# The router product with the router's columns stationary, and the dense lists made anew

## The chip, the cores and the metric

One Trainium2 chip; the kernel runs on one of its NeuronCores. The metric is the device time of one execution in microseconds. TensorE multiplies, VectorE, ScalarE and GpSimd (POOL in the profile) do the elementwise work, SyncE (SP) issues most DMAs. Each engine takes its instructions strictly in the order of its own program and waits at semaphores for the others.

## The reference

Two transformer layers over x of 4 x 1024 tokens and 256 columns, all float32, here cut to what matters:

```
xn = layernorm(x)
x1 = x + attention0(xn) + relu(xn @ W1 + b1) @ W2 + b2      # the dense stage: 4 batches
xn = layernorm(x1)
scores = softmax(xn @ Wg.T)                                  # the router: 256 -> E = 8 logits a token
weights, experts = top_k(scores, 2); weights /= weights.sum()
moe = sum over the 2 chosen experts of weight * LoRA-SwiGLU(xn, expert)
out = x1 + grouped_attention1(xn) + moe
```

The router's logits decide which rows go to which expert, so the rows are scattered into slots, sorted by expert, before the experts run.

## The kernel before

The program has four stages: dense (stage 0), the first half of the second layer's attention (1), the experts (2), and the second half of the attention (3). What each engine does is cut into *units*, such as `RL:2`, and each engine has a list of them: `LAYER0_UNITS` for the dense stage, `ATTENTION_UNITS` for the attention. The dense lists are cyclic. `layer0_order` goes through a list once per turn, for turns -1 to 4; a unit with no mark belongs to the batch of the turn, one with `+` to the next batch, one with `-` to the one before. So the units with `+`, all in the last part of the list, open the kernel in turn -1. Between two stages the lists are joined: `AHEAD` says how many units of the next stage go behind each named unit of the last batch. No engine looks past a unit that waits.

TensorE's dense units: `XT` turns two tiles of xn; `PT` the product of wq.wk with xn; `VV` values of two tiles; `S` scores of one tile, `TP` turned probabilities, `AV` probabilities by values, `LT` and `FC` the output product; `W1` (16 per batch) and `W2` (8 per batch) the FFN; `EP` half of an expert's LoRA fold. `RT` turns two tiles of the second layernorm's output, `RL` makes the router's logits of these two tiles. Each `x + y` product that is not the router's is made of three fp32r products of high and low parts (helper `times`, L549). The turned tiles go through two PSUM banks T, the products through four banks G, in the order of TensorE's list: a bank can be written again when the unit that used it four products before has been evicted.

The router's path in a pair of tiles: VectorE's `N1` normalizes two tiles (L934) when GpSimd's `X1` has its root; TensorE's `RT` turns them (L709); ScalarE's `RT` copies the bank to `xn1T` (L726), which is a single buffer, when TensorE has finished the previous `RL`; TensorE's `RL` (L718) makes four f32 products, for each tile and each of the two column blocks, with the turned tile stationary and the router's 8 columns moving; VectorE's `RL` copies 16 columns to `logit` and finds the top two (L955 to L961). `TK` and `TG` make indices and gates, `CH` in stage 1 counts the slots.

At the start, GpSimd's `FA` splits an expert's LoRA factors, which SP's `LL` has loaded; SP's `LL:1` waits for `FA:0`. In the first batch `FA:1` goes on with the low parts of the two FFN weights: W1's (L523, signal `ffn_split` 1), then W2's (L525, signal 2). TensorE's `W1:0` of the first batch waits for signal 1, ScalarE's `W1:0` for signal 2. GpSimd's `XT` adds a bias row to two tiles (L517). SP's `CL` clears three slots with zeros (385.5 KB, 24 in all), which must be over before the scatter.

At the join, GpSimd's `ES` makes the low part of a folded expert matrix (L532) from ScalarE's `EL`, SP's `SM` stores the matrix (L457), `SX` and `SN` store x1 and xn. SP's `LC:1` loads the rotation table `turn` (L1273) behind the last `SM`; VectorE's `OF:0` (L1611) waits for it. In stage 1 GpSimd's `SC` scatters one tile of rows to the slots with two indirect DMAs (L1347), `YS` takes a root for an output tile when VectorE has its variance, `LE` loads the first expert.

## Time and profile before

| | |
|---|---|
| median of 3 runs | 1117.2 us (1113.53 to 1121.52) |
| the profiled execution | 1116.3 us, span 1114.6 us |
| mean granted clock | 0.974 of full speed |
| TensorE busy | 1055.8 us, 95% of the span |
| VectorE busy | 781.8 us, 70% |
| GpSimd busy | 434.6 us, 39% |
| ScalarE busy | 393.5 us, 35% |
| chain that ended last | TensorE 87%, VectorE 4% |

A busy TensorE is one that has a product in flight; the ends of products are modelled. In the chain of waits, "issue" and "another core or an unknown queue" are time for which the profile shows no releaser. The granted clock has two levels, full (2.4 GHz) and half (1.2 GHz); a value between them is a stretch that had both. The kernel is one long sequence, so a stretch of the span is a stage: dense to about 430 us, the first attention half to about 620, the experts to about 970, the second half to the end.

### The profile page before, as it was taken

What the parts mean: (1) busy time and instruction counts of PE and PEld (TensorE: products, weight loads), DVE (VectorE), ACT (ScalarE), POOL (GpSimd) and SP (SyncE); (2) the same over time, 40 slices, a digit from 0 to 9 for tenths busy, and PEclk for the clock granted to TensorE, in tenths of its full rate; (3) what the DMA queues carried; (4) which work ended last, traced back from release to release, by engine and by line L of the source; (5) the groups of instructions that cost most, each with busy time, mean ns of one, the idle gap of its engine ahead of it and who ended that gap; (6) DMA issues with size and microseconds to landing.
All of it is one profiled execution on the core that took longest, in us unless ns stands there. A gap on an engine that the chain in (4) does not pass through costs nothing.

```text
span 1114.6 us, 20433 instructions
## 1 busy us (share of the span) xinstructions
PE 1055.8 (95%) x6338; PEld 915.2 (82%) x6338; DVE 781.8 (70%) x1741; ACT 393.5 (35%) x770; POOL 434.6 (39%) x416
## 2 busy tenths in 40 slices
PE   5999999999999996995899899999999999999995
PEld 4899999999999996864677788888888888877874
DVE  5688787878788676754565777777777777764745
ACT  2636463555446363431211222222222222442300
POOL 2846454555447331045575100000011010088886
PEclk8999999999999998897899999999999999999998
DMA  9364672666468346425466446534355252265456
GB/s 272 97 206 130 187 244 101 192 160 202 140 190 205 123 148 185 126 76 171 151 189 214 166 136 223 171 116 142 101 194 166 78 194 58 84 123 86 68 95 141
DMA packets 113780, 168.61 MB, mean 151 GB/s; under 512 B 17296, under 2 KB 87568, under 8 KB 113552
## 3 DMA queue, kind: packets, MB, share of 16 engines
q1 hardware_dynamic: 93328, 120.09, 35.5%
q0 software_dynamic: 20352, 47.23, 15.3%
...
## 4 chain that ended last, share of the span: by engine, by line
PE 87%; DVE 4%; issue 2%; another core or an unknown queue 2%; DMA 2%; SPq 1%; POOL 1%; ACT 0%; DVEq 0%; POOLq 0%; ACTq 0%
PE wide L549 19%; PE wide L1900 17%; PE bank L549 11%; PE bank L1900 9%; PE wide L1398 7%; PE bank L1398 3%; PE bank L1925 3%; PE wide L1458 3%; PE wide L1482 2%; PE bank L1482 2%; PE bank L640 1%; PE bank L1893 1%; PE wide L1471 1%; PE wide L1468 1%
## 5 line engine op out<-in xcount | busy, mean ns | idle before, releaser
L1900 PE MATMUL wide<-expert_ring,xsT 128*128 x642 | 170.5, 401 | 3.1 <-DVE xsT L1989 2.3
L1900 PEld LDWEIGHTS wide<-expert_ring,xsT 128*128 128x128 f32 x642 | 113.3, 188 | 23.4 <-issue 3.9
L1958 ACT ACTIVATE gsT<-bank 128x512 fp32r<-128x512 f32 x71 | 42.5, 599 | 242.3 <-PE bank L1925 242.3
...
L2001 DVE TENSOR_TENSOR slots_h<-wide,expert_bias 128x512 f32<-128x512 f32 x71 | 49.1, 691 | 68.0 <-PE wide L1900 67.8
L1347 POOL DMA_INDIRECT slot_rows_scratch<-ring,slot x64 | 69.2, 1081 | 52.0 <-DVE slot L1734 32.0
L532 POOL TENSOR_TENSOR folded_matrix<-fold,folded_matrix 128x512 fp32r<-128x512 f32 x48 | 64.0, 1341 | 42.5 <-ACT folded_matrix L726 39.7
L549 PE MATMUL wide<-xnT,w 128*128 128x512 f32 x234 | 60.3, 399 | 0.0
L1900 PEld LDWEIGHTS bank<-expert_ring,gsT 128*128 128x128 f32 x432 | 56.1, 189 | 3.5 <-issue 0.3
L944 DVE TENSOR_TENSOR hT<-hid,hT 128x512 fp32r<-128x512 f32 x64 | 54.6, 860 | 5.9 <-ACT hid L781 5.1
L549 PE MATMUL wide<-xnT,pT 128*128 128x512 f32 (+2 forms) x288 | 58.6, 348 | 0.0
L529 POOL TENSOR_TENSOR rsa<-vea,half 128x1 f32<-128x1 f32 x32 | 21.3, 666 | 95.3 <-DVE vea L908 94.3
L1900 PE MATMUL bank<-expert_ring,xsT 128*128 x210 | 57.5, 409 | 0.1
L1900 PE MATMUL bank<-expert_ring,gsT 128*128 x432 | 57.3, 281 | 0.1
L1900 PEld LDWEIGHTS wide<-expert_ring,gsT 128*128 128x128 f32 x420 | 54.2, 188 | 3.0
L1989 DVE TENSOR_TENSOR gsT<-bank,gsT 128x512 fp32r<-128x512 f32 x71 | 49.1, 691 | 9.9 <-ACT gsT L1958 0.5
L549 PE MATMUL wide<-w,hT 128*128 128x256 f32 x456 | 55.7, 278 | 0.0
L1330 POOL DMA_INDIRECT first_half<-slot_results_scratch,slot x32 | 51.9, 1622 | 9.2 <-issue 9.2
L1900 PE MATMUL wide<-expert_ring,gsT 128*128 x420 | 55.2, 280 | 0.0
L2010 DVE SCALAR_TENSOR_TENSOR slots_g<-slots_h,xs_ring,slots_h 128x512 f32<-128x512 f32 x71 | 53.4, 752 | 2.5
L549 PEld LDWEIGHTS wide<-w,hT 128*128 128x128 f32 x456 | 54.5, 188 | 0.4
L1330 POOL DMA_INDIRECT x1b<-slot_results_scratch,slot x16 | 26.0, 1626 | 73.4 <-DVE x1b L1650 68.9
...
## 6 DMA issues: line engine op xcount, KB each, us to landing
...
slot_rows_scratch<-zeros SPq DMA_DIRECT2D x23, 385.5 KB, 7.5
...
```

The costliest lines, as they stand in the source:

```text
L532: tt(fold_part(n, 1), fold[:, n % 2, :], fold_part(n, 0), ALU.subtract).then_inc(matrix_ready, 1)
L549: ins = mm(o, stationary(i), moving(j), start=(first and q == 0), stop=(last and q == 2))
L944: tt(hT[:, 1, n % IC, :], hid[:, n % 2, :], hT[:, 0, n % IC, :], ALU.subtract).then_inc(hid_low, 1)
L1330: nc.gpsimd.indirect_dma_start(out=target, out_offset=None, in_=scr["ys"], in_offset=index(k, tile_at), bounds_check=SLOTS - 1, compute_op ...
L1347: nc.gpsimd.indirect_dma_start(out=scr["xs"], out_offset=index(k, n), in_=ring[:, n % RINGS, k * ROW:(k + 1) * ROW], in_offset=None, bound ...
L1398: ins = mm(o, stationary(i), moving(j), start=(first and k == 0), stop=(last and k == 2))
L1482: last = mm(o[:, 0:DIM], oT[:, h % 2, e, n % 4 * P:(n % 4 + 1) * P], wo1[:, e, :], start=(e == 0), stop=(e == EC - 1))
L1900: ins = mm(o, parts[i], moving, start=(first and q == 0), stop=(last and q == 2))
L1958: return nc.scalar.activation(o, i, ACT.Copy)
L1989: tt(flat[1], bank, flat[0], ALU.subtract).then_inc(taken, 1)
L2001: tt(h1[:, j % 2, :], H[j % 2][0], bias(e, 0, HID), ALU.add).then_inc(h1_ready, 1)
L2010: stt(out=g[:, i, :], in0=h1[:, i, :], scalar=xs[:, j % ROUND, DIM:ROW], in1=h3[:, i, :], op0=ALU.mult, op1=ALU.mult).then_inc(g_ready, 1)
```

## The change

RT now lays the turned tiles by column block, both tiles side by side. RL makes two f32 products, each with 8 of the router's columns stationary and the two turned tiles (256 columns) moving; the result is 8 x 256, logits turned. ScalarE has a new unit RL: it copies these to `xn1T`'s first 8 partitions. TensorE has a new unit RB: it turns them back, two blocks of 8 x 128, into columns 256 to 271 of the same bank. VectorE's RL and ScalarE's next RT wait for RB instead of RL. All dense lists, the lists of the first attention half and the joins have a new order: `W1:0+` stands eighth among the units that open TensorE's program (it was seventeenth), the clears move from one turn before to one turn behind their batch, GpSimd's first YS stands behind SC:7 instead of SC:10. The diff (of the attention lists only GpSimd's is shown):

```diff
--- before.py
+++ after.py
@@ -47,34 +47,35 @@
 
 LAYER0_UNITS = {
     "tensor": """
-        RL:3- W1:6 S:5 FC:1 LT:2 EP:4 W1:7 AV:3 TP:4 FC:2 S:6 EP:5 W2:0 LT:3 AV:4 W2:1 TP:5 FC:3 W2:2 EP:6 W2:3
-        LT:4 W1:8 EP:7 AV:5 TP:6 S:7 W1:9 W1:10 FC:4 LT:5 W1:11 W1:12 AV:6 TP:7 EP:8 W1:13 W1:14 W1:15 FC:5 LT:6
-        XT:0+ EP:9 AV:7 EP:10 XT:1+ FC:6 W2:4 LT:7 EP:11 W2:5 VV:0+ PT:0+ W2:6 PT:2+ EP:0+ XT:2+ FC:7 W2:7 XT:3+
-        RT:0 VV:1+ EP:1+ S:0+ RL:0 S:1+ RT:1 PT:1+ VV:2+ TP:0+ PT:3+ RL:1 W1:0+ S:2+ RT:2 AV:0+ TP:1+ W1:1+ S:3+
-        LT:0+ W1:2+ EP:2+ RL:2 W1:3+ AV:1+ TP:2+ VV:3+ EP:3+ S:4+ RT:3 FC:0+ W1:4+ LT:1+ W1:5+ AV:2+ TP:3+
+        W1:4 LT:1 AV:2 W1:5 FC:1 TP:3 LT:2 EP:2 S:5 W1:6 EP:3 AV:3 TP:4 W1:7 FC:2 S:6 EP:4 LT:3 AV:4 W2:0 EP:5
+        TP:5 W2:1 FC:3 W2:2 LT:4 EP:6 RL:3- AV:5 RB:3- W2:3 TP:6 EP:7 W1:8 FC:4 W1:9 S:7 W1:10 W1:11 LT:5 W1:12
+        AV:6 TP:7 EP:8 W1:13 W1:14 W1:15 FC:5 LT:6 EP:9 AV:7 XT:0+ W2:4 XT:1+ FC:6 W2:5 VV:0+ LT:7 EP:10 W2:6
+        XT:2+ FC:7 W2:7 PT:0+ XT:3+ EP:11 PT:2+ RT:0 W1:0+ EP:0+ VV:1+ S:0+ RL:0 EP:1+ RT:1 VV:2+ RB:0 S:1+ PT:1+
+        TP:0+ S:2+ W1:1+ AV:0+ PT:3+ RL:1 TP:1+ RT:2 S:3+ RB:1 W1:2+ LT:0+ AV:1+ RL:2 RT:3 W1:3+ RB:2 VV:3+ TP:2+
+        S:4+ FC:0+
     """,
     "scalar": """
-        W1:5 TP:3 EL:3 W1:6 LT:2 EX:5 W1:7 TP:4 EL:4 LT:3 EL:5 TP:5 LT:4 EX:6 W1:8 TP:6 EL:6 EL:7 W1:9 W1:10 LT:5
-        EX:7 W1:11 W1:12 TP:7 W1:13 W1:14 EL:8 LT:6 W1:15 XT:0+ EL:9 XT:1+ LT:7 VV:0+ GX:0- EL:10 PT:0+ EL:11
-        PT:2+ XT:2+ XT:3+ RT:0 VV:1+ EL:0+ EX:0+ RT:1 PT:1+ TP:0+ VV:2+ PT:3+ EX:1+ W1:0+ EL:1+ RT:2 TP:1+ W1:1+
-        EX:2+ W1:2+ LT:0+ EX:3+ TP:2+ W1:3+ VV:3+ RT:3 EL:2+ LT:1+ W1:4+ EX:4+
+        W1:3 LT:1 W1:4 EX:4 TP:3 W1:5 LT:2 EL:2 W1:6 EX:5 TP:4 W1:7 LT:3 EL:3 TP:5 EL:4 EX:6 RL:3- EL:5 LT:4 TP:6
+        W1:8 W1:9 EL:6 EL:7 W1:10 LT:5 EX:7 W1:11 W1:12 TP:7 W1:13 W1:14 W1:15 LT:6 XT:0+ XT:1+ EL:8 EL:9 LT:7
+        VV:0+ GX:0- XT:2+ PT:0+ EL:10 XT:3+ PT:2+ RT:0 EL:11 W1:0+ VV:1+ RL:0 EX:0+ RT:1 VV:2+ TP:0+ PT:1+ EX:1+
+        EL:0+ W1:1+ RL:1 TP:1+ PT:3+ RT:2 EX:2+ W1:2+ LT:0+ RL:2 RT:3 EX:3+ EL:1+ VV:3+ TP:2+
     """,
     "vector": """
-        AV:2 W1:4 RL:3- W1:5 TP:3 S:5 FC:1 LT:2 EP:4 SA:2 W1:6 W1:7 TP:4 ST:0+ AV:3 SA:3 ST:1+ FC:2 S:6 EP:5 LT:3
-        AV:4 W2:0 ST:2+ W2:1 TP:5 FC:3 W2:2 EP:6 ST:3+ VA:0+ LT:4 EP:7 W2:3 SA:4 AV:5 X1:0 TP:6 W1:8 S:7 SA:5
-        FC:4 W1:9 LT:5 W1:10 NM:0+ W1:11 AV:6 W1:12 EP:8 TP:7 SA:6 W1:13 W1:14 FC:5 LT:6 EP:9 W1:15 TK:0- XT:0+
-        AV:7 EP:10 X1:1 SA:7 FC:6 W2:4 XT:1+ LT:7 EP:11 NM:1+ W2:5 N1:0 VV:0+ PT:0+ N1:1 W2:6 EP:0+ PT:2+ XT:2+
-        X1:2 FC:7 W2:7 TG:0- XT:3+ X1:3 S:0+ VV:1+ S:1+ EP:1+ RL:0 PT:1+ N1:2 TP:0+ VV:2+ PT:3+ RL:1 S:2+ AV:0+
-        W1:0+ N1:3 SA:0+ TP:1+ S:3+ EP:2+ RL:2 W1:1+ LT:0+ AV:1+ F1:0 W1:2+ TP:2+ EP:3+ VV:3+ FC:0+ W1:3+ S:4+
-        SA:1+ LT:1+
+        VV:3 TP:2 S:4 FC:0 LT:1 AV:2 SA:2 W1:3 FC:1 EP:2 W1:4 TP:3 LT:2 S:5 W1:5 AV:3 W1:6 ST:0+ EP:3 TP:4 W1:7
+        SA:3 FC:2 LT:3 AV:4 F1:0- EP:4 SA:4 S:6 ST:1+ W2:0 EP:5 TP:5 W2:1 FC:3 W2:2 EP:6 ST:2+ LT:4 ST:3+ RL:3-
+        X1:0 AV:5 W2:3 VA:0+ EP:7 TP:6 W1:8 FC:4 S:7 NM:0+ W1:9 W1:10 LT:5 SA:5 W1:11 AV:6 EP:8 W1:12 TP:7 W1:13
+        TK:0- W1:14 FC:5 W1:15 NM:1+ LT:6 EP:9 SA:6 X1:1 XT:0+ AV:7 W2:4 SA:7 FC:6 W2:5 XT:1+ LT:7 EP:10 VV:0+
+        TG:0- W2:6 FC:7 XT:2+ N1:0 X1:2 W2:7 N1:1 PT:0+ EP:11 PT:2+ EP:0+ X1:3 XT:3+ S:0+ W1:0+ VV:1+ EP:1+ RL:0
+        S:1+ VV:2+ TP:0+ PT:1+ N1:2 AV:0+ N1:3 S:2+ W1:1+ TP:1+ PT:3+ RL:1 S:3+ SA:0+ LT:0+ AV:1+ SA:1+ RL:2
+        W1:2+
     """,
     "gpsimd": """
-        ES:2 SA:1 ES:3 SA:2 FA:4 SA:3 ES:4 ES:5 SA:4 FA:5 ES:6 VA:0+ ES:7 XT:0+ SA:5 SA:6 ES:8 FA:0+ ES:9 X1:0
-        SA:7 X1:1 ES:10 ES:11 X1:2 X1:3 FA:1+ XT:1+ ES:0+ XT:2+ ES:1+ FA:2+ XT:3+ SA:0+ F1:0 FA:3+
+        FA:2 SA:2 FA:3 ES:2 ES:3 XT:2 SA:3 FA:4 ES:4 ES:5 XT:3 SA:4 VA:0+ ES:6 FA:5 ES:7 SA:5 FA:0+ F1:0- XT:0+
+        X1:0 SA:6 ES:8 ES:9 XT:1+ X1:1 SA:7 ES:10 X1:2 ES:11 X1:3 FA:1+ ES:0+ SA:0+ ES:1+ SA:1+
     """,
     "sync": """
-        LX:0+ LW:2 LW:3 SM:1 LL:4 LL:5 LW:4 SM:2 CL:0+ SX:0 SM:3 CL:1+ LW:5 LL:0+ CL:2+ CL:3+ SM:4 CL:4+ LW:0+
-        LL:1+ SM:5 SX:1 LL:2+ SN:0 SG:0- LW:1+ SM:0+ LL:3+ CL:5+ SN:1
+        LX:0+ SM:0 LW:2 LL:3 CL:0- LL:4 SM:1 LW:3 LW:4 LL:5 SM:2 SX:0 CL:1- LW:5 CL:2- LL:0+ SM:3 CL:3- SM:4
+        LW:0+ SX:1 LL:1+ CL:4- SM:5 CL:5- SN:0 LL:2+ LW:1+ SN:1 SG:0-
     """,
 }
 
@@ -339,7 +340,8 @@
     nmx = sb("nmx", [P, 2])
     rsum = sb("rsum", [P, 4])
     rinv = sb("rinv", [P, 4])
-    xrT = sb("xn1T", [P, 2, DC, P])
+    xrT = sb("xn1T", [P, DC, 2 * P])
+    turned_logits = xrT[0:E, 0, :]
     logit = sb("logit", [P, TPB, E])
     top = sb("top", [P, TPB, 8])
     topi = sb("topi", [P, TPB, 8], mybir.dt.uint32)
@@ -362,6 +364,7 @@
     gates_ready, gates_stored, diff_ready, ed_ready = (sem("gates_ready"), sem("gates_stored"), sem("diff_ready"),
                                                        sem("gate_exponents_ready"))
     varn_ready, r2_ready, g_step = sem("xn1_var_ready"), sem("r2_ready"), sem("gate_step")
+    logits_high, logits_done = sem("turned_logits_ready"), sem("logits_done")
     matrix_out, matrix_ready = sem("matrix_out"), sem("matrix_parts_ready")
     factors_ready = sem("factors_ready")
     p_step, p_held, v_held = sem("gpsimd_step"), keep["held"]["gpsimd"], keep["held"]["vector"]
@@ -706,18 +709,22 @@
                 o, done = t_free(u)
                 for t in range(2):
                     for c in range(DC):
-                        last = tr(o[:, (DC * t + c) * P:(DC * t + c + 1) * P], xb[:, b % 2, 2 * n + t, c * P:(c + 1) * P],
+                        last = tr(o[:, (2 * c + t) * P:(2 * c + t + 1) * P], xb[:, b % 2, 2 * n + t, c * P:(c + 1) * P],
                                   ident[:])
                 last.then_inc(done, 1)
             elif kind == "RL":
                 pe.wait_ge(late_in, 32)
                 pe.wait_ge(*taken_t((b, "RT", n)))
                 o, done = g_free(u)
+                for c in range(DC):
+                    last = mm(o[0:E, 0:2 * P], rout[:, c, :], xrT[:, c, :], start=(c == 0), stop=(c == DC - 1))
+                last.then_inc(done, 1)
+            elif kind == "RB":
+                pe.wait_ge(logits_high, TPB // 2 * b + n + 1)
                 for t in range(2):
-                    for c in range(DC):
-                        last = mm(o[:, t * E:(t + 1) * E], xrT[:, t, c, :], rout[:, c, :],
-                                  start=(c == 0), stop=(c == DC - 1))
-                last.then_inc(done, 1)
+                    last = tr(g_bank((b, "RL", n))[:, 2 * P + t * E:2 * P + (t + 1) * E], turned_logits[:, t * P:(t + 1) * P],
+                              ident[0:E, 0:E])
+                last.then_inc(logits_done, 1)
 
         return unit
 
@@ -782,8 +789,10 @@
             elif kind == "RT":
                 if TPB // 2 * b + n:
 
-                    act.wait_ge(g_done, G_AT[(b, "RL", n - 1) if n else (b - 1, "RL", TPB // 2 - 1)] + 1)
-                copy(xrT[:].rearrange("p t c q -> p (t c q)"), t_of(u)[:]).then_inc(taken_t(u)[0], 1)
+                    act.wait_ge(logits_done, TPB // 2 * b + n)
+                copy(xrT[:].rearrange("p c q -> p (c q)"), t_of(u)[:]).then_inc(taken_t(u)[0], 1)
+            elif kind == "RL":
+                copy(turned_logits, g_of(u)[0:E, 0:2 * P]).then_inc(logits_high, 1)
             elif kind == "GX":
                 act.wait_ge(diff_ready, b + 1)
                 if b:
@@ -951,8 +960,9 @@
                     dve.wait_ge(matrix_ready, q - 1)
                 tt(fold[:, n % 2, :], raw[:, m % 2, n % 2 * 512:(n % 2 + 1) * 512], o, ALU.add).then_inc(taken_g(u)[0], 1)
             elif kind == "RL":
-                o, pair = g_full(u), (2 * n, 2 * n + 1)
-                nc.vector.tensor_copy(logit[:, 2 * n:2 * n + 2, :].rearrange("p t e -> p (t e)"), o[:, 0:2 * E]).then_inc(taken_g(u)[0], 1)
+                o, pair = g_bank(u), (2 * n, 2 * n + 1)
+                dve.wait_ge(logits_done, TPB // 2 * b + n + 1)
+                nc.vector.tensor_copy(logit[:, 2 * n:2 * n + 2, :].rearrange("p t e -> p (t e)"), o[:, 2 * P:2 * P + 2 * E]).then_inc(taken_g(u)[0], 1)
                 hold(dve, v_held, *taken_g(u))
                 for t in pair:
                     last = nc.vector.max(top[:, t, :], logit[:, t, :])
...
     "gpsimd": """
-        SC:0 SC:1 SC:2 SC:3 SC:4 SC:5 SC:6 SC:7 SC:8 SC:9 SC:10 YS:0 LE:0 YS:1 SC:11 YS:2 SC:12 SC:13 SC:14 SC:15
-        SC:16 YS:3 SC:17 YS:4 SC:18 SC:19 SC:20 SC:21 YS:5 SC:22 YS:6 SC:23 YS:7 SC:24 SC:25 SC:26 LE:1 SC:27
-        SC:28 YS:8 LE:2 SC:29 SC:30 SC:31 YS:9 YS:10 YS:11 YS:12 YS:13 YS:14 YS:15
+        SC:0 SC:1 SC:2 SC:3 SC:4 SC:5 SC:6 SC:7 YS:0 SC:8 SC:9 SC:10 SC:11 SC:12 SC:13 SC:14 LE:0 SC:15 SC:16
+        SC:17 YS:1 YS:2 LE:1 SC:18 YS:3 SC:19 SC:20 YS:4 SC:21 YS:5 SC:22 YS:6 SC:23 YS:7 SC:24 SC:25 LE:2 SC:26
+        SC:27 SC:28 YS:8 SC:29 SC:30 SC:31 YS:9 YS:10 YS:11 YS:12 YS:13 YS:14 YS:15
     """,
...
@@ -1075,9 +1085,9 @@
 
 AHEAD = (
 {
-    "tensor": "W2:6:1 RT:0:1 RT:1:3 RT:2:1 RT:3:2",
-    "scalar": "LT:7:2 EL:10:1 EL:11:1 RT:0:3 RT:1:2 RT:2:1 RT:3:3",
-    "vector": "X1:2:2 W2:7:2 RL:0:2 N1:2:2 RL:1:1 N1:3:3 F1:0:2 TK:0:1",
+    "tensor": "FC:7:1 RT:0:1 RT:1:1 RB:0:1 RT:2:1 RT:3:1 RL:3:2",
+    "scalar": "LT:7:4 EL:10:1 RL:0:1 RT:1:1 RT:2:1 RL:2:2 RL:3:3",
+    "vector": "W2:5:1 EP:10:1 X1:2:1 X1:3:1 N1:3:4 RL:1:4 F1:0:1 TK:0:5",
     "gpsimd": "",
     "sync": "LW:5:1 SM:5:1",
 },
@@ -1085,7 +1095,7 @@
     "tensor": "YY:14:1 YY:15:29",
     "scalar": "GA:15:18",
     "vector": "YS:13:1 YS:14:2 YF:11:1 YS:15:4 YF:12:19 YF:13:1 YF:15:2",
-    "gpsimd": "YS:10:1 YS:13:1",
+    "gpsimd": "YS:12:1 YS:14:1",
     "sync": "RG:31:12",
 },
 {
```

The units that open the kernel, from these lists, and the join on VectorE and SP (`[1]` is stage 1, `3.` the last batch):

```
TensorE before: XT:0 XT:1 VV:0 PT:0 PT:2 EP:0 XT:2 XT:3 VV:1 EP:1 S:0 S:1 PT:1 VV:2 TP:0 PT:3 W1:0 S:2 AV:0 TP:1 W1:1
TensorE after:  XT:0 XT:1 VV:0 XT:2 PT:0 XT:3 PT:2 W1:0 EP:0 VV:1 S:0 EP:1 VV:2 S:1 PT:1 TP:0 S:2 W1:1 AV:0 PT:3 TP:1
GpSimd before:  VA:0 XT:0 FA:0 FA:1 XT:1 ES:0 ...     after: VA:0 FA:0 XT:0 XT:1 FA:1 ES:0 ...
SP before:      LX:0 CL:0 CL:1 LL:0 CL:2 CL:3 CL:4 LW:0 LL:1 ...     after: LX:0 LL:0 LW:0 LL:1 ...
VectorE join before: 3.W2:7 [1]WL:0 [1]OF:0 2.TG:0 3.X1:3 3.RL:0 [1]WL:1 [1]UT:1 3.N1:2
VectorE join after:  3.W2:7 3.N1:1 3.EP:11 3.X1:3 [1]OF:0 3.RL:0 3.N1:2 3.N1:3
SP join before: 3.SM:4 3.SM:5 [1]LC:1 3.SX:1 3.SN:0 2.SG:0 3.SN:1 3.SG:0
SP join after:  3.SX:1 2.CL:4 3.SM:5 [1]LC:1 2.CL:5 3.SN:0 3.SN:1 2.SG:0 3.CL:0 ... 3.CL:5 3.SG:0
```

## Rows read from the trace of the kernel before

**Rows 1.** Busy time by stretch, whole kernel; busy us and count per engine, clock, DMA.
```profile
100.00:200.00 100.00, 100.00 (x701) 92.98 (x700) 79.54 (x213) 49.92 (x99) 49.89 (x50) 1.00 0.54 169
440.00:450.00 10.00, 5.37 (x24) 4.97 (x25) 9.29 (x30) 1.39 (x3) 0.69 (x1) 0.50 0.54 128
500.00:510.00 10.00, 3.83 (x14) 2.91 (x14) 3.79 (x6) 0.00 (x0) 7.40 (x8) 0.67 0.73 204
510.00:520.00 10.00, 3.54 (x18) 2.60 (x17) 1.22 (x3) 2.37 (x5) 4.62 (x5) 0.84 0.59 176
520.00:530.00 10.00, 10.00 (x41) 8.05 (x41) 7.70 (x14) 2.16 (x5) 5.39 (x5) 0.80 0.47 155
550.00:560.00 10.00, 7.76 (x24) 6.28 (x25) 8.69 (x17) 4.13 (x7) 2.11 (x3) 0.66 0.27 70
```

**Rows 2.** Instructions in order, TensorE; start, length, what, idle before.
```profile
443.70 1.12 PE L709 MATMUL bank<-ident,u 128*128 128x128 f32 x4 [8.07 <-DVE u L934]
```

**Rows 3.** What TensorE waited for: us in total, times, longest.
```profile
PE bank L1482 <- issue: 6.2, 1, 6.2
PE wide L1398 <- DVE uT L1619: 4.7, 1, 4.7
PE bank L1482 <- DVE oT L1668: 3.8, 1, 3.8
```

**Rows 4.** Chain of waits, 130 to 180 us; start, us, what.
```profile
130.20 0.79 PE wide L718 x8
135.00 0.11 PE bank L640
135.11 1.38 PE bank L549 x6
```

**Rows 5.** Chain of waits, from 1000 us: another f32 product.
```profile
1016.18 1.73 PE bank L1482 x8
```

**Rows 6.** Instructions in order, GpSimd, start of the kernel.
```profile
16.24 1.52 POOL L517 TENSOR_TENSOR u<-u,crow 128x256 f32<-128x256 f32 x2 [3.71 <-DVE crow L824]
24.32 1.43 POOL L500 TENSOR_TENSOR lora_parts<-lora,lora_parts 32x512 fp32r<-32x512 f32 x1 [0.18 <-POOL lora_parts L499]
32.53 4.60 POOL L523 TENSOR_TENSOR w<-u,w 128x2048 fp32r<-128x2048 f32 x1 [0.26 <-POOL lora_parts L500]
37.10 4.65 POOL L525 TENSOR_TENSOR w<-w_raw,w 128x2048 fp32r<-128x2048 f32 x1
```

**Rows 7.** Instructions in order, TensorE, start of the kernel.
```profile
22.22 2.90 PE L549 MATMUL bank<-wv,xnT 128*128 128x256 f32 x12 [1.21 <-DVE xnT L843]
37.19 1.66 PE L549 MATMUL bank<-xnT,w 128*128 128x512 f32 x6 [0.62 <-POOL w L523]
41.70 1.54 PE L549 MATMUL wide<-xnT,pT 128*128 128x512 f32 x6
```

**Rows 8.** Instructions in order, ScalarE, start of the kernel.
```profile
41.85 0.69 ACT L780 ACTIVATE hT<-bank,cols 128x512 fp32r<-128x512 f32 x1 [4.19 <-POOL w L525]
```

**Rows 9.** Chain of waits, start of the kernel: SP and the LoRA load.
```profile
12.10 0.91 SPq L462
13.98 8.11 DMA lora<-in_expert_lora
```

**Rows 10.** Instructions in order, VectorE, start of the kernel.
```profile
22.59 2.03 DVE L872 TENSOR_SCALAR xp<-u,mv,rs 128x256 f32<-128x256 f32 x4
```

**Rows 11.** Instructions in order, VectorE, join: eviction of the last W2 unit.
```profile
429.53 0.42 DVE L920 TENSOR_TENSOR u<-u,wide 128x256 f32<-128x256 f32 x1 [1.02 <-PE wide L549]
```

**Rows 12.** Chain of waits, 400 to 640 us, at the join.
```profile
427.31 1.38 POOL folded_matrix L532
428.70 0.54 SPq L457
429.34 7.45 DMA turn<-in_turn
```

**Rows 13.** Costliest groups of the page: busy, mean ns, idle before.
```profile
L1347 POOL DMA_INDIRECT slot_rows_scratch<-ring,slot x64 | 69.2, 1081 | 52.0 <-DVE slot L1734 32.0
```

28 lines of the change are left out of this document (14 added, 14 removed).

## The prediction

> **What bounds the kernel now.** I read the busy shares of the engines by stretch first. From 100 to 200 us, well inside the dense stage, TensorE is busy for all of the 100 us at full clock while the other engines have room [rows 1], and I take that stretch for the whole middle of the dense stage. There only TensorE's own work counts: whatever adds to it is paid, and whatever other engines get more of is not, until it makes TensorE wait. Then I read its waits. Nearly all idle time lies at the edges: 8.1 us before the router's third turned pair of the last batch [rows 2], and 6.2, 4.7 and 3.8 us in the attention half behind it [rows 3]. After the first of these the granted clock is at half (1.2 GHz) in 440 to 450 us, and it is down again around the others [rows 1]. A new order of the dense lists can therefore gain only at the edges, and can lose anywhere.
>
> **The router's product.** Before, a unit RL is four f32 products, each moving 8 columns and loading 128 x 128: 8 records, 0.79 us in the chain of waits in mid-stage [rows 4]. The new RL is two products moving 256 columns, so 4 records. The nearest row is another f32 product of 256 moving columns: 8 records in 1.73 us, 0.216 each [rows 5]. Four make 0.86 us. The new RB turns two 8 x 128 blocks back. Bound from above: a 128 x 128 turn takes 0.11 us [rows 4], two are 0.22; from below: nothing. I take 0.20, because the loaded block still has 128 columns like that row. A unit goes from 0.79 to 1.06, +0.27; twelve units lie in the full stretch, **+3.2 us** (+0.9 to +3.5). The last four lie in the join, counted there. ScalarE gets 16 small copies; it is half idle in mid-stage [rows 1], so I cost them at nothing there; were that cover gone, the 0.3 to 0.6 us of each would stand in front of the next turned pair. VectorE's work is unchanged.
>
> The Trainium skill, "TensorE: Matmul & The Clock Gate", section on the back-to-back issue gap, gives 262 cycles for 256 columns, 0.109 us at 2.4 GHz, with no surcharge for f32. By that the product would cost 0.44 us. The trace's f32 row disagrees by a factor of two, and I go by the trace.
>
> **The start of the dense stage** is the largest term. A unit W1 of the first batch needs the low part of the first FFN weight, which GpSimd makes (L523, 32.53 us, 4.60 long), and ScalarE's W1 unit needs the second one too (L525, from 37.10, 4.65 long) [rows 6]. Before, W1:0 is seventeenth in TensorE's list; the engine comes to it at about 36.6 and starts at 37.19, barely late [rows 7]. ScalarE waits for the second part until 41.85 [rows 8], while TensorE goes on with what was ahead. In the new lists W1:0 stands eighth, right behind PT:2, on both queues. Behind it, in order, are now EP:0, VV:1, S:0, EP:1, VV:2, S:1, PT:1, TP:0 and PT:3, all of which ran ahead of it.
>
> When does the gate open? SP no longer issues two clears of the slots ahead of the first LoRA load. That load went out at 13.98 and landed 8.1 us later, at 22.1; the clears took SP from 12.10 [rows 9]. So it goes out 1.9 us earlier and has the data of two clears less ahead of it; I take a landing at 19.7 (18.0 to 20.5). FA:0 takes 3.7 us (22.1 to the end of L500 at 25.8), so to 23.4. Now both bias units (1.52 each) stand between FA:0 and FA:1: 26.4; one of them used to fill the wait ahead of FA:0 [rows 6]. FA:1 takes about as long as FA:0 less its queue time, 3.3, then L523: the first gate opens at 34.5 instead of 37.1, the second at 39.1 instead of 41.8.
> When does TensorE come to it? VectorE now normalizes the second half of the tiles (2.03 us, L872 [rows 10]) ahead of the first turned tiles, which moves VV:0 from 22.22 [rows 7] to about 24. VV:0, XT:2, PT:0, XT:3, PT:2 end near 30.2. So it idles 4.3 us there. Six records of 512 columns are 1.38 us in mid-stage [rows 4], twelve of 256 as many columns: W1:0, EP:0, VV:1, S:0, EP:1 (1.4, 0.24, 1.4, 0.7, 0.24) run to 38.5. VV:2 needs the bank that W1:0 filled, which ScalarE empties only at 39.1 + 1.3 = 40.4. From there VV:2, S:1, PT:1, TP:0, S:2, W1:1, AV:0, PT:3 and TP:1 are 8.1 us: 48.5. Before, the same set was done at 41.70 [rows 7]. The difference, **+6.7 us** (+4 to +9, by the landing and by whether the idling halves the clock), meets a stage with no idle time, so nothing gives it back.
>
> **The join with the attention half.** What SP does there matters. The last EP unit now stands behind W2:7, whose eviction on VectorE starts at 429.53 [rows 11], and ScalarE takes it behind RT:0; the split on GpSimd takes 1.38 [rows 12]. The last store of the expert matrix, 428.70 before, then goes out near 433.9, and the load of the rotation table, queued behind it, at 434.5 instead of 429.34. It took 7.45 us to land [rows 12]; so 441 to 442 instead of 436.8. VectorE's OF:0 waits for it with N1:2 and N1:3 queued behind, and the third RT waits for N1:2 as before. From that landing to the third RT VectorE needed 6.9 us (436.8 to 443.70 [rows 2, 12]); the gates, X1:3, a weight's low part and a UT unit no longer stand in between, which leaves 3.9 by my estimate: 445.4, 1.7 us later. RB:2 adds a step on the way to the last RT's copy and RL, 0.6 us, and UT:2 now runs after the wait, in the slow clock. **+3 us** (0 to +6). Six clears of the last batch move in front of its gates' store on SP; they are hidden behind the logits, unless the queue is still full there.
>
> **The scatter.** GpSimd's indirect writes, 1.08 us each [rows 13], ran 22 in a row before its first YS; the new list has 16, with YS:0 then holding GpSimd until the first output rows are there. In that burst TensorE, ScalarE and VectorE stand still with no releaser on record [rows 3]. I read it as other queues starved by the burst, but no row shows that. Bounds: all of the standing still goes (-21, below) or it grows by half as much (+8). I take **-2**, close to nothing since a shorter burst sometimes only moves the stall.
>
> **The sum**: 3.2 + 6.7 + 3 - 2 = +10.9 on the profiled execution's 1116.3 us, 1127. The median of the runs is 1117.2, so on that I am 0.9% slower.
>
> **Rivals.**
> - *The standing still in the scatter goes.* TensorE is busy for 3.83 and 3.54 us of the two stretches from 500 to 520 and 7.76 of 550 to 560 [rows 1]: 14.9 us idle. What it did there ran at clocks of 0.67, 0.84 and 0.66, and 10 us behind it at 0.80: 1.3 + 0.6 + 2.6 + 2.0 = 6.5 us more, 21 together. 1116.3 + 12.9 - 21 = 1108. This is the end on the other side, not slower, and it decides if the new position of YS:0 comes before the engines run dry. For it: each pause of GpSimd's burst is followed by a restart. Against: GpSimd's burst begins at about the same place.
> - *The start gate does not bite*, because the first LoRA load lands near 17 and its factors are done before TensorE arrives: 1116.3 + 3.2 + 3 - 2 = 1120.5. For it, the queue ahead of it shrinks; against, GpSimd has two more bias units in the way.
> - *The product is cheap.* If a product of 256 columns costs what an fp32r one of as many columns does (half of 1.38 / 6, 0.115), RL and RB are 0.66 us, 0.13 less than before: -1.6 instead of +3.2, 1122. It is what the skill's section above gives.
> - *The turn-back stalls mid-stage.* ScalarE's copy of the next turned pair waits for RB, and RB stands behind a whole VV:2, S:3 or W1:3. For 1.4 us ScalarE holds everything queued behind that copy. If TensorE runs out of evicted banks for 1 us per unit, twelve units cost +12: 1139. Against it, ScalarE's half idle time.
>
> **How the numbers follow.** The forecast's case (1119 to 1135 alone) has 0.42, the scatter 0.20, the open gate 0.15, the cheap product 0.07, the turn-back 0.16. What a measurement can tell from no change is about 1%, so 1106 to 1128. Slower by more: 0.2 of the forecast's case, 0.15 of the turn-back, 0.02 else: 0.37. Faster by more: half of the scatter's case less what sits inside, and what the new attention lists may bring beside it: 0.16. The rest 0.47. The range runs from the scatter's case to just under the turn-back's.
>
> **What would show it.** The product's line with four records and about 0.216 us each; two short records for the turning back. TensorE waiting on GpSimd's L523 or on W1's bank between 30 and 41 us, with W1:0 first and not after PT:3. The wait before the third RT at 9 to 10 us. TensorE busy for all of 60 to 430 still; idle time there is the fourth rival. The first long gap in the scatter shorter. It is wrong if the dense stage ends no later than before.

## The result, and the profile after

The changed kernel takes 1129.2 us, the median of 4 runs (1127.01 to 1130.52); the kernel before, beside it, 1119.0 (1113.53 to 1121.52). The ratio is 1.0104, with a 95% interval of 1.0085 to 1.0124. The forecast was 1127, in a range from the scatter's case (1108) to just under the turn-back's (1139). The profiled execution took 1128.95 us, with a span of 1127.2, against 1116.3 and 1114.6 before: 12.6 us of span to account for.

Busy time by stretch of the changed kernel, with the columns of [rows 1]:

```profile
20.00:30.00 10.00, 6.31 (x25) 5.75 (x26) 5.39 (x9) 5.87 (x8) 8.60 (x10) 0.66 0.13 45
30.00:40.00 10.00, 6.53 (x30) 5.52 (x29) 2.67 (x4) 1.80 (x4) 9.45 (x3) 0.83 0.25 82
100.00:200.00 100.00, 100.00 (x689) 89.28 (x688) 77.74 (x211) 48.50 (x99) 46.51 (x50) 1.00 0.46 152
450.00:460.00 10.00, 2.69 (x8) 0.70 (x7) 1.03 (x2) 2.03 (x5) 1.22 (x2) 0.81 0.85 273
460.00:470.00 10.00, 6.36 (x25) 4.16 (x25) 8.68 (x27) 3.46 (x7) 0.00 (x0) 0.50 1.13 259
```

The middle of the dense stage is still all TensorE, at full clock; the opening is now half idle and runs partly at 1.2 GHz (clock 0.66 and 0.83); the join from 450 us is poorer than [rows 1] showed it at 440. What TensorE waited for (us in total, times, longest), to be held against [rows 3]:

```profile
PE bank L712 <- DVE u L943: 10.5, 2, 10.0
PE wide L1408 <- issue: 4.2, 5, 2.1
PE bank L552 <- DVE xnT L852: 3.8, 1, 3.8
PE wide L552 <- POOL w L526: 3.5, 1, 3.5
PE bank L1423 <- issue: 2.9, 1, 2.9
```

Two of these waits lie in the opening. The one for the turned tiles (L852) was 1.21 us before [rows 7], the one for the weight's low part (L526) 0.62. The long waits behind the join, 6.2, 4.7 and 3.8 us, have become 4.2 in five pieces, 2.9, and 2.5 that ended with VectorE.

**The start**, instructions in order (start, length, what, idle before). They answer to [rows 6 to 8]:

```profile
23.69 2.90 PE L552 MATMUL bank<-wv,xnT 128*128 128x256 f32 x12 [3.81 <-DVE xnT L852]
30.57 4.53 POOL L526 TENSOR_TENSOR w<-u,w 128x2048 fp32r<-128x2048 f32 x1 [0.26 <-POOL lora_parts L503]
35.15 1.90 PE L552 MATMUL wide<-xnT,w 128*128 128x512 f32 x6 [3.47 <-POOL w L526]
39.80 0.69 ACT L787 ACTIVATE hT<-wide,cols 128x512 fp32r<-128x512 f32 x1 [7.48 <-POOL w L528]
41.21 1.60 PE L552 MATMUL wide<-wv,xnT 128*128 128x256 f32 x12 [0.25 <-ACT hid L788]
```

W1:0 starts at 35.15 with 3.47 us of idle time before it, and VV:2 at 41.21, when ScalarE has emptied W1:0's bank. The fourth score tile of batch 0, for which the same set of units has been done in both kernels, starts at 49.13 against 41.70 [rows 7]: **+7.4**. That is one profile against one. The six kernels that open exactly like the one before start this tile between 41.70 and 43.05, four of the five with the new opening between 49.13 and 49.48 and the fifth at 50.53, so a start is known to about 1 us.

**The stage** from there to the end of the last W2 unit (the start of TensorE's next record) takes 395.3 us (49.13 to 444.45) against 387.6 (41.70 to 429.33): **+7.7**. Kernels with the same lists and product repeat this length within 0.02 us. The new product and the turn back from 100 to 400 us, by shape (busy, mean ns, idle):

```profile
L720 PE MATMUL bank<-xn1T,router 128*8 128x256 f32 x24 | 6.2, 380 | 0.0
L725 PE MATMUL bank<-ident,xn1T 8*128 8x8 f32 x12 | 1.7, 212 | 0.0
L725 PEld LDWEIGHTS bank<-ident,xn1T 8*128 8x128 f32 x12 | 1.2, 135 | 2.2 <-issue 2.2
```

**The join.** TensorE in order, and the chain of waits (start, us, what):

```profile
462.69 1.11 PE L712 MATMUL bank<-ident,u 128*128 128x128 f32 x4 [10.00 <-DVE u L943]
466.15 1.87 PE L720 MATMUL wide<-xn1T,router 128*8 128x256 f32 x4 [0.73 <-issue]
```

```profile
449.29 1.28 POOL folded_matrix L535
450.59 0.55 SPq L460
451.24 7.67 DMA turn<-in_turn
```

The third turned pair waits 10.00 us, and the product behind it 0.73. The profile names no releaser for the 0.73; ScalarE's copy of the pair (465.45, 0.60 long) lies in it, and that copy had waited for the turn back, a step that the old product did not have. The pair starts 18.2 us behind the last W2 unit, 14.4 before [rows 2]. From that unit to the first product of an expert's weights it is 184.4 us against 187.2: **-2.8**. From there to TensorE's last product it is the same, 485.4 and 485.2. 7.4 + 7.7 - 2.8 is 12.3 of the 12.6; the rest lies behind.

Those 184.4 us hold a loss and a gain. Up to the first scatter they are 64.1 us against 57.3, with TensorE idle for 12.8 us against 9.0. From the first scatter to the experts they are 120.3 against 130.0, with the columns of [rows 1], the kernel before first:

```profile
486.59:616.57 129.98, 110.53 (x493) 83.94 (x492) 68.00 (x149) 22.61 (x40) 81.58 (x83) 0.92 0.57 174
508.54:628.86 120.32, 108.13 (x491) 80.71 (x490) 67.68 (x149) 20.37 (x34) 80.19 (x83) 0.97 0.62 188
```

TensorE's idle time there falls from 19.5 us to 12.2, and its mean granted clock rises from 0.92 to 0.97.

### The profile page after: what moved, and what is told of

Same layout as the page of the kernel before. It is cut to its first block, busy times and chain, and to the rows that moved or that the text cites. A ratio compares the mean times of both kernels' runs of the same rounds, so it can differ in the third digit from the quotient of the medians.

```text
span 1127.2 us, 20384 instructions
## 1 busy us (share of the span) xinstructions
PE 1066.7 (95%) x6306; PEld 906.2 (80%) x6306; DVE 776.4 (69%) x1741; ACT 397.6 (35%) x786; POOL 430.2 (38%) x416
## 3 DMA queue, kind: packets, MB, share of 16 engines
q0 software_dynamic: 20352, 47.23, 15.1%
## 4 chain that ended last, share of the span: by engine, by line
PE 89%; DVE 3%; issue 3%; POOL 2%; DMA 1%; SPq 1%; ACT 0%; DVEq 0%; POOLq 0%; ACTq 0%
PE wide L552 17%; PE wide L1910 17%; PE bank L552 13%; PE bank L1910 9%; PE wide L1408 7%; PE bank L1408 3%; PE bank L1935 3%; PE wide L1468 2%; PE wide L1492 2%; PE wide L1481 2%; PE wide L1478 2%; PE bank L1492 2%; PE bank L643 1%; PE bank L1903 1%; PE wide L720 1%
## 5 line engine op out<-in xcount | busy, mean ns | idle before, releaser
L552 PE MATMUL wide<-xnT,w 128*128 128x512 f32 x216 | 56.0, 398 | 3.5 <-POOL w L526 3.5
L552 PE MATMUL bank<-w,hT 128*128 128x256 f32 x480 | 59.1, 279 | 0.0
L1910 PE MATMUL bank<-expert_ring,gsT 128*128 x432 | 57.3, 281 | 0.1
L552 PEld LDWEIGHTS bank<-w,hT 128*128 128x128 f32 x480 | 56.8, 188 | 0.1
L552 PEld LDWEIGHTS wide<-xnT,pT 128*128 128x128 f32 x288 | 47.6, 189 | 6.3
```

Source lines behind the costliest of these rows:

```text
L552: ins = mm(o, stationary(i), moving(j), start=(first and q == 0), stop=(last and q == 2))
L1910: ins = mm(o, parts[i], moving, start=(first and q == 0), stop=(last and q == 2))
```

## The experiments

The kernel before gave 1117.5 us beside the first four kernels, 1100.7 beside the next four and 1101.4 beside the last four; these were three different chips. So every ratio is to the kernel before on the same chip, and stages are compared by their own length. "The rest" of a kernel is what it has over the kernel before, by its ratio, when the start and the stage of its profile are taken off; it is known no better than the start.

**1. The opening turn in its old order.**

```
+START = {"tensor": "XT:0 XT:1 VV:0 PT:0 PT:2 EP:0 XT:2 XT:3 VV:1 ... PT:3 W1:0 S:2 ...", "scalar": ..., "vector": ...}
     for turn in range(-1, BATCH + 1):
+        if turn < 0 and opening:
+            order += [(0, u.split(":")[0], int(u.split(":")[1])) for u in opening]
+            continue
```

> The changed kernel, but its opening turn (the units of batch 0 that run ahead of the first full turn) stands on TensorE, ScalarE and VectorE in the order of the kernel before; the rest of the lists and the new router product stay. Theory A (the start is the gate of the feed-forward weights, met too early): TensorE no longer waits 3.5 us on the low split of the weights, its 24 products of the first hidden tile no longer run at the low clock, and the same set of units is done about 7 us earlier; the time falls by 7 us to about 1122, a ratio of 1.003 to 1.005 to the kernel before. Rival B (TensorE's later units wait for the same VectorE and ScalarE work anyway, the gate only hides it): the time falls by 2 us at most, ratio 1.008 or more.

1122.16 us, ratio 1.0037 (1.0021 to 1.0053): 7.5 us under the changed kernel (1.0104 less 1.0037, of 1117.5). Its busy time in the opening:

```profile
20.00:30.00 10.00, 8.14 (x40) 6.89 (x40) 7.99 (x14) 7.25 (x9) 8.81 (x10) 0.83 0.11 36
30.00:40.00 10.00, 10.00 (x67) 9.20 (x66) 6.65 (x15) 6.38 (x16) 9.87 (x3) 1.00 0.25 84
```

The fourth score tile starts at 41.69, the stage takes 395.4. What the opening loses, nothing behind it gives back. Theory A holds, rival B falls.

**2. W1:0 alone moved back** (on TensorE, ScalarE and VectorE; TensorE's list is shown).

```
-"... XT:3 PT:2 W1:0 EP:0 VV:1 S:0 EP:1 VV:2 S:1 PT:1 TP:0 S:2 W1:1 ..."
+"... XT:3 PT:2 EP:0 VV:1 S:0 EP:1 VV:2 S:1 PT:1 TP:0 S:2 W1:0 W1:1 ..."
```

> The changed kernel with one unit moved: the first hidden tile W1:0 of the opening turn goes behind the third score row, just ahead of W1:1, on TensorE, ScalarE and VectorE. Theory A (that unit's gate alone makes the start late): within 1.5 us of the kernel whose whole opening turn is as before, so about 6 to 7 us under the changed kernel. Rival B (the start is late for its whole order, the transposes and pattern products placed ahead of the values): 3 us or less of gain. Rival C (ScalarE's wait on the second half of the split, not TensorE's, is what matters, and W1:0 is still reached before it ends): gain of 3 to 5 us.

1126.08 us, ratio 1.007 (1.0053 to 1.0087). The fourth score tile starts at 43.52: 5.6 of the 7.4 us are back, and 1.8 stay, against the old order's 41.69. TensorE's first values in this kernel, and then in that of experiment 1:

```profile
23.84 2.90 PE L564 MATMUL bank<-wv,xnT 128*128 128x256 f32 x12 [3.42 <-DVE xnT L864]
```

```profile
23.02 1.82 PE L564 MATMUL bank<-wv,xnT 128*128 128x256 f32 x12 [1.86 <-DVE xnT L864]
```

Half of the 1.8 us and more are here: VectorE normalises the second half of the tiles ahead of the first turned ones, TensorE waits 3.42 in place of 1.86, and the twelve products behind that wait take 2.90 in place of 1.82, at a granted clock of 0.53 in place of 0.83 from 20 to 30 us. The length of the twelve is not all of it: in experiment 3, with the old order, they also take 2.90, and the fourth score tile still starts at 41.94. In the start itself the gate is three quarters of the loss and the order the rest, between theory A and rival B. The median gained only 3.8 us of the 5.6, a size inside rival C's 3 to 5. But C's mechanism is not there: no wait of TensorE or ScalarE from 15 to 60 us ends with GpSimd. The interval is 2 us wide on each side, and what ate the remainder is not shown.

**3. The new product in the old lists.** The code of the changed kernel; the old lists with RB in TensorE's and RL in ScalarE's. VectorE's RL units stand one to four places later, and ScalarE's RT:1 one later.

```
-RT:0 VV:1+ EP:1+ S:0+ RL:0 S:1+ RT:1 PT:1+ VV:2+ TP:0+ PT:3+ RL:1 W1:0+ S:2+ RT:2 ...
+RT:0 VV:1+ EP:1+ S:0+ RL:0 S:1+ RT:1 PT:1+ RB:0 VV:2+ TP:0+ PT:3+ RL:1 W1:0+ S:2+ RB:1 RT:2 ...
```

> The kernel before with its own lists and only the new router product: the columns of the router stationary, two turned tiles moving, the ScalarE copy and the turn back put into the old lists two to four units behind their product. Theory A (the product costs TensorE 0.37 us more for each of 12 pairs of tiles in the stage, and latency in the tail): 4.4 us in the stage and 1 to 3 us behind it, 5 to 7 us in all, ratio 1.004 to 1.006. Rival B (the turn back stalls TensorE, or slows its neighbours, so the stage grows by the whole 7.7 us that the changed kernel shows): ratio 1.008 or more. Rival C (the product is free beside other work): ratio 1.000 to 1.002.

1125.12 us, ratio 1.0072 (1.0055 to 1.009), so 8.0 us. The fourth score tile starts at 41.94 and the stage takes 396.3, **+8.7**. In the stage that is rival B's size; the ratio lies between theory A's 1.006 and B's 1.008. B's first cause is not there, since TensorE waits for nothing in the stage; that leaves its second, slower neighbours.

**4. The new lists with the old product.** The code of the kernel before; the new lists without RB on TensorE and RL on ScalarE.

> The changed kernel with the router product of the kernel before: the new lists without the turn-back unit on TensorE and the copy unit on ScalarE. Theory A (the cost of the new product is its own and adds to that of the lists): 5 to 7 us under the changed kernel, about 1123, and the stage still 3.3 us longer than before outside the router's rows. Rival B (the 3.3 us outside the router's rows come with the new product, by shared banks or by the small stationary tiles): 8 us or more under the changed kernel, 1121 or less. Rival C (the lists carry the whole loss): within 2 us of the changed kernel.

1120.82 us, ratio 1.0026 (1.0007 to 1.0044): 8.7 us under the changed kernel. The stage takes 386.5 us, 1.2 less than before. So rival B again: the whole growth of the stage, 8.9 us with these lists, comes with the product. In the stage this kernel and the changed one have the same 2,624 other matmul records in the same order, so each can be held against its twin. TensorE in order around the first unit of batch 1, here and then in the changed kernel:

```profile
138.09 0.87 PE L550 MATMUL wide<-xnT,pT 128*128 128x256 f32 x6
138.79 0.95 PE L719 MATMUL wide<-router,xn1T 128*128 128x8 f32 x8
139.60 0.49 PE L696 MATMUL wide<-lora_parts 96*128 96x512 f32 x1
139.93 0.60 PE L710 MATMUL bank<-ident,u 128*128 128x128 f32 x4
140.28 1.62 PE L550 MATMUL bank<-wv,xnT 128*128 128x256 f32 x12
141.74 0.87 PE L550 MATMUL wide<-xnT,pT 128*128 128x256 f32 x6
142.45 0.86 PE L550 MATMUL bank<-xnT,wqk_product 128*128 128x512 f32 x3
```

```profile
137.85 0.87 PE L552 MATMUL wide<-xnT,pT 128*128 128x256 f32 x6
138.65 1.03 PE L720 MATMUL wide<-xn1T,router 128*8 128x256 f32 x4
139.61 0.50 PE L698 MATMUL wide<-lora_parts 96*128 96x512 f32 x1
139.95 0.60 PE L712 MATMUL bank<-ident,u 128*128 128x128 f32 x4
140.30 1.66 PE L552 MATMUL bank<-wv,xnT 128*128 128x256 f32 x12
141.89 0.29 PE L725 MATMUL wide<-ident,xn1T 8*128 8x8 f32 x2
142.11 0.98 PE L552 MATMUL wide<-xnT,pT 128*128 128x256 f32 x6
142.92 0.40 PE L552 MATMUL bank<-xnT,wqk_product 128*128 128x512 f32 x1
```

Read starts, not lengths; a row can hold several records, and their lengths overlap. The six products ahead of the router's take 0.70 us in one kernel and 0.80 in the other; the router's 0.81 and 0.96; the twelve ahead of the turn back 1.46 and 1.59; the turn back itself 0.22; the six behind it 0.71 and 0.81. Summed over the twelve units from each record's start to the next one's: the router's own four records 11.5 us against 9.7, the turn back 2.6, and then time that belongs to no line of the router, called a seam here: 1.08 us just ahead of the product, 1.14 just ahead of the turn back, 1.28 just behind it, 0.23 just behind the product, and 0.7 thinly over all the rest. That is the 8.9.

The product's own 11.5 us hide one more seam. Its first three records take 0.216 to 0.220 us each, and only the fourth takes longer, 0.31 from its start to the next record (139.61 above):

```profile
139.30 0.38 PE L720 MATMUL wide<-xn1T,router 128*8 128x256 f32 x1
```

So the 0.240 of a mean record is not how long such a record takes. Four at 0.217 make 10.4 us, 0.7 over the old product, and 1.1 us are a seam at the product's end. The f32 product of [rows 5], also with 256 moving columns but with 128 stationary ones, has no such end: all eight of its records take 0.216 to 0.219, and the record ahead of it 0.111 like the ones before that. Behind it stands a turn of 128x128, as behind six of the router's twelve products, whose last records all take 0.31; ahead of it stand f32 products, not fp32r. The old router product, full width and between the same fp32r neighbours as the new one, shows no long record at either end. Both point at the 8 stationary columns; no run changes them alone.

A row of the new-lists kernel gives the measure for what stands behind a turn back. It shows the second and third of the twelve records that begin at 140.28, behind the four full-size turns of L710:

```profile
140.48 0.40 PE L550 MATMUL bank<-wv,xnT 128*128 128x256 f32 x2
```

The first of the twelve takes 0.20 us, the others 0.12. In this kernel the first record of 256 columns behind any turn of 128x128 takes 0.20 us, where one between its own kind takes 0.11 to 0.12; two such turns take 0.13 to 0.14 by their own starts and pass some 85 ns on.

**5. The turn back at full height.** It takes whole 128x128 blocks, of which rows 0 to 7 are logits and the rest leftovers; VectorE reads 8 columns of each.

```
-last = tr(g_bank(...)[:, 2 * P + t * E:2 * P + (t + 1) * E], turned_logits[:, t * P:(t + 1) * P], ident[0:E, 0:E])
+last = tr(g_bank(...)[:, (2 + t) * P:(3 + t) * P], xrT[:, 0, t * P:(t + 1) * P], ident[:])
```

> The changed kernel with one thing else: the turn back takes whole 128x128 blocks (the 8 rows of logits and 120 rows of leftovers beneath them, against the whole identity) and VectorE picks the 8 columns of each block, so no instruction of it has 8 rows. In the changed kernel the record just before a turn back is 95 ns longer, and the one just after it 106 ns longer, than the same record with the same lists and the old product: 2.4 us over 12 pairs. Theory C (the seam belongs to the change of height, 8 rows between products of 128): the seams go, the two transposes take 0.11 us each as now, the stage shortens by about 2.4 us to 393, the time to about 1126. Rival D (the seam belongs to any transpose placed there, or to what waits on the copy): the stage stays within 0.5 us of 395.3. Rival E (128 columns out in place of 8 cost more than they save): the stage is 1 us or more longer.

1117.20 us, ratio 1.0147 (1.0125 to 1.0169), on another chip; the stage took 392.25 us, 3.1 less than the changed kernel's. It was run once more beside the changed kernel:

> The changed kernel with the turn back over whole 128x128 blocks, once more, now beside the changed kernel itself. Theory C (the seams around the 8-row instructions are the cost): the stage again 3.1 us shorter than the changed kernel's, the whole 2 to 4 us faster. Rival K (what the stage gives is lost again in the second stage): within 1 us of the changed kernel in the whole.

1117.16 us against the changed kernel's 1120.77, and again 392.25 us of stage: 3.6 us faster in the whole. The same place in its trace:

```profile
141.71 1.66 PE L552 MATMUL bank<-wv,xnT 128*128 128x256 f32 x12
143.21 0.38 PE L725 MATMUL wide<-ident,xn1T 128*128 128x128 f32 x2
143.34 0.95 PE L552 MATMUL wide<-xnT,pT 128*128 128x256 f32 x6
144.14 0.62 PE L552 MATMUL bank<-xnT,wqk_product 128*128 128x512 f32 x2
```

The twelve ahead take 1.50, the turn back of 128 columns 0.13 in place of 0.22 for 8, the six behind it still 0.80. Over twelve units the seam ahead fell from 1.14 to 0.05 us, the turn back from 2.6 to 1.6, the thin remainder from 0.7 to nothing; the seam behind only from 1.28 to 1.02. Theory C is right for the seam ahead and for the thin remainder. Behind, 85 of the 106 ns stay, but they are the 85 ns that every full-size turn here passes on (experiment 4), so a price of the turn and not of its height; the 8 rows add 21. With its neighbours a full-size turn back costs 0.23 us a unit, the one with 8 rows 0.42. A stationary operand of full width for the router's product was not tried, so the seams ahead of that product and at its end, 1.08 and 1.1 us, have no shown cause.

The Trainium skill, "TensorEngine Tiling (Array Packing)", Key Properties, says that changing the tiling mode, as opposed to the tile, drains TensorE. If a block of 8 rows, or one of 8 columns, takes another mode, that rule puts a drain on each side. The seams ahead of both agree with it (95 and 90 ns, the first gone at full height), and so does the one at the product's end (93 ns and 20 behind); behind the turn back only 21 ns hang on the height. Which mode an instruction takes is in no row.

**6. GpSimd's new list of the second stage alone.**

```
-SC:0 ... SC:7 SC:8 SC:9 SC:10 YS:0 LE:0 YS:1 SC:11 YS:2 ...
+SC:0 ... SC:7 YS:0 SC:8 SC:9 ... SC:14 LE:0 SC:15 SC:16 SC:17 YS:1 YS:2 ...
```

> The kernel before with one list exchanged: GpSimd's of the second stage, in which the first layer-norm power YS:0 stands behind 8 scatters and not 11, and the next ones later. By the medians the new lists win 3 to 4 us between the end of the feed-forward products and the experts (with the old product too), though the first scatter is issued later. Theory F (those gains come from GpSimd's place for YS:0, which ScalarE's and TensorE's later work waits for): 3 us faster, ratio 0.996 to 0.998. Rival G (they come from the order on TensorE, VectorE and ScalarE): within 1 us of the kernel before. Rival H (the later powers hold VectorE up): slower by 2 us.

1109.30 us, ratio 1.0081 (1.0058 to 1.0104), so 8.9 us slower. Theory F falls, and the loss is over four times what rival H gave. What waited from 480 to 615 us:

```profile
DVE vey L1679 <- POOL rsy L1339: 15.2, 1, 15.2
PE wide L1398 <- DVE v L1645: 14.5, 1, 14.5
```

VectorE stood 15.2 us for one power that was queued behind scatters, and TensorE 14.5 for VectorE.

**7. All new lists of the second stage, the rest as before.**

> The kernel before with all lists of the second stage exchanged for the new ones, the first stage's lists and the old product kept (VectorE's units at the join one earlier in one place and four later in another, as the new order asks). Theory F2 (the new second-stage lists carry the gain whatever precedes them): 3 to 4 us faster than the kernel before, about 1114, ratio 0.9965. Rival G2 (the gain needs the later join, because the scatters then meet fewer instructions in flight): within 1.5 us of the kernel before. Start and first stage are to stay at 41.7 and 387.6 us in both.

1096.28 us, ratio 0.9961 (0.9944 to 0.9977), and once more on the third chip:

> The kernel before with all lists of the second stage exchanged for the new ones, once more: on the second chip it was faster by 0.4 per cent. Theory F2: faster here too, 3 to 6 us, ratio 0.995 to 0.9975. Rival G2 (it was that chip alone): within 1 us.

1096.86 us, ratio 0.9951 (0.9929 to 0.9974): 4.3 and 5.4 us faster than the kernel before, with a stage of 387.6 in both. Theory F2 holds, G2 falls. **This kernel beats both.** Its third turned pair (in order, from the second of the two runs):

```profile
441.75 1.11 PE L709 MATMUL bank<-ident,u 128*128 128x128 f32 x4 [4.62 <-DVE u L934]
```

That is 11.3 us behind the last W2 unit (430.47), where the kernel before has 14.4.

**8. VectorE's OF units late, in the kernel before.** The counts in `AHEAD` change with the list, so that both stand behind N1:3.

```
-SD:0 UT:0 WL:0 OF:0 WL:1 UT:1 OF:1 FB:0 UT:2 WL:2 FB:1 FB:2 UT:3 ...
+SD:0 UT:0 WL:0 WL:1 UT:1 FB:0 UT:2 WL:2 OF:0 OF:1 FB:1 FB:2 UT:3 ...
```

> The kernel before with VectorE's two sums OF:0 and OF:1, which wait for the turned positions from memory, moved behind the last normalised rows of the first stage (N1:3), so that the last turned tiles of the router no longer stand behind a 7.5 us transfer. Theory I (the join sets the first scatter, and that the end): the last router product ends 4 to 8 us earlier, the first scatter 3 us earlier or more, and the time falls by 3 us, ratio 0.997. Rival J (the scatters are not short of time, the second stage's own products are late instead by what OF is late): within 1.5 us, or slower.

1101.52 us, ratio 1.0008 (0.999 to 1.0027), and its first scatter goes out 58.5 us behind the last W2 unit, 1.2 later than before. The join theory falls; the outcome is rival J's, by another way than it gave. VectorE, ahead of the third turned pair:

```profile
443.04 0.74 DVE L934 TENSOR_SCALAR u<-u,mv,rs 128x256 f32<-128x256 f32 x2 [6.28 <-DMA x_scratch<-u]
```

The rows are normalised in place, so they wait for the store of the old ones, which SP issues behind the same turn load. The wait for the load had covered a second one, and the third pair still starts 13.2 us behind the last W2 unit (430.68), against 14.4.

**9. The changed kernel on the third chip.**

> The changed kernel as it is, beside the three below. The kernel before ran at 1117.5 us beside the first four experiments and at 1100.7 beside the next four, and its start and first stage, by the nearest kernels, did not move, so the second stage's scatters set what a chip gives. If this chip is like the first, the ratio is 1.010 again; if it is like the second, where fewer stalls are left to win back, the changed kernel loses the start (7.7 us) and the stage (7.7 us) and wins back little: 1.013 to 1.017.

1120.77 us, ratio 1.0173 (1.0144 to 1.0202), the upper case of the expectation. From the first scatter to the experts, here and then in experiment 8's kernel on the second chip, which differs from the kernel before in the place of two of VectorE's units and took as long:

```profile
509.93:620.73 110.80, 105.00 (x490) 79.77 (x490) 67.52 (x149) 20.37 (x34) 79.79 (x83) 0.98 0.68 204
489.13:601.11 111.98, 106.38 (x493) 81.20 (x492) 67.50 (x149) 22.85 (x40) 80.02 (x84) 0.97 0.66 202
```

TensorE is idle for 5.8 and 5.6 us of them, where the first chip gave 19.5 before and 12.2 after the change. Where hardly any standing still is left, the change wins 1 us of it and not 10. Experiment 8's kernel also shows where the chips differ: its start and stage are not shorter, and from the last W2 unit to the experts it takes 170.4 us, not 187.2.

**10. As 7, with GpSimd's old list.**

> As the kernel with all second-stage lists exchanged, but GpSimd keeps its list of before, which alone, exchanged, cost 0.8 per cent. Theory L (the lists fit each other: GpSimd's order of powers and scatters is made for the order in which VectorE makes the variances): slower than with all lists exchanged, and no faster than the kernel before, ratio 1.000 or more. Rival M (GpSimd's new list is a loss wherever it stands, the gain is in the other three): faster than with all lists exchanged, ratio under 0.994.

1102.13 us, ratio 1.0009 (0.9992 to 1.0025). By the times theory L holds: GpSimd's list is worth 5 us among the others and costs 9 without them. VectorE's waits do not show why. At L1683 it waits 15.7 us for powers here and 9.8 with all lists new, but at L1679 2.0 and 8.3, together 17.7 and 18.1. What the 5 us are is open.

**The join, split.** GpSimd's first scatter, counted from the end of the last W2 unit (us):

| kernel | first scatter | end of last W2 | between |
|---|---|---|---|
| before | 486.59 | 429.33 | 57.3 |
| changed | 508.54 | 444.45 | 64.1 |
| new lists, old product (4) | 500.03 | 435.83 | 64.2 |
| old lists, new product (3) | 496.61 | 438.26 | 58.4 |
| all new second-stage lists (7, first run) | 485.04 | 430.09 | 55.0 |
| the same (7, second run) | 483.50 | 430.47 | 53.0 |

The rest, as defined above, is -3.5 us for the changed kernel, -3.7 in experiment 1, -3.6 with the new lists and the old product, and -0.9 with the new product in the old lists: what the second stage wins comes with the lists. The dense lists carry the lateness of the first scatter, the product about 1 us of it, and the attention lists by themselves would have gained 2 to 4.

## Why the prediction was right, and where it was not

The time, 1129.2, is 2 us from the forecast; it is slower by 1.04%, just past the bound, a case that I gave 0.37. But the sum of +10.9 met +11.6 (1.0104 of 1117.5) because errors cancelled: a product and a join that cost more, a scatter that won more. That the time came out so close is luck.

- **What bounds the kernel** held: TensorE was busy for all of the stage, every microsecond added to it was paid, and the start was not given back (experiment 1).
- **The router's product** failed as a size: +3.2 forecast, +8.7 (experiment 3) and +8.9 (experiment 4) measured, over twice the upper end of 3.5. What was priced came true. The records took 0.217 us as forecast (0.216), +0.7 us over twelve units where I had +0.9, and the turn back's own two took 0.215 a unit where I had 0.20, 2.6 for 2.4. The rest, 5.6 us, was not in the working at all: I priced the new records and none of the seams that they make. 4.9 us of it are the five seams (1.08 ahead of the product, 1.1 in its last record, 0.23 behind it, 1.14 ahead of the turn back, 1.28 behind it), 0.7 lie thinly over the stage. The upper bound of 0.22 for the two turns holds for full-size blocks, 0.23 with their neighbours; with 8 rows it was 0.42.
- **The cheap product** is out: the records take 0.217 us and not 0.115. The Trainium skill, "TensorE: Matmul & The Clock Gate", section on the back-to-back issue gap, gives 262 cycles for 256 columns, 0.109 us at 2.4 GHz, and has no line for f32. For records of an f32 product the trace disagrees here as it did before.
- **The start**: +6.7 forecast (the two times there, 48.5 and 41.70, make 6.8), +7.4 measured, within its range. The first gate opened at 35.1 (34.5 forecast), the second at 39.7 (39.1), VV:0 started at 23.69 (24). What I left at the edge of the range, the clock, came: 0.66 and 0.83. Experiment 2 splits it, 5.6 to the gate and 1.8 to the new order without it.
- **The join**: +3 forecast; the first scatter is 6.8 us later, past the range's end of 6. The turn load went out at 451.24, 6.8 us behind the last W2 unit (5.2 forecast), and 3.9 us of that reached the third turned pair (1.7 forecast). The lists' part by experiment 4 is 6.9 us.
- **The scatter**: -2 forecast. Start and stage are +15.1 and the whole is +11.6, so join and scatter together gave -3.5. In the profiles the stretch from the first scatter to the experts is 9.7 us shorter, **about 10**, of which 7.3 is TensorE's idle time. Part of the rest is work that it had already done when the scatter began 6.8 us later. That mechanism was my first rival, at half its size of 21. It is also why the time looks well forecast. On the third chip there was almost nothing of it to win: 19.1 us slower (1.0173), where start and stage make about 15 and the join costs its 7 (the sum of single profiles is 2 us over the medians here). My rival's place for it, the one unit YS:0, was wrong: alone, GpSimd's list cost 9 us (experiment 6). And [rows 3] does not say that all engines stood with no releaser: it does so for 6.2 us, while the waits of 4.7 and 3.8 ended with VectorE.
- **The turn-back rival** is out in its own form, since TensorE never waited on ScalarE in the stage. Its result of a longer stage came all the same, by the seams.

**Open**: the cause of the seams ahead of the router's product and at its end, where the rows point at the 8 stationary columns; how 8 rows of a turn back come to cost 0.7 us spread thinly over the stage; why the new second-stage lists gain only together; what on a chip sets how long the engines stand during the scatters. That it is the chip at all rests on one block of runs on each.
